# Expert tiles of a mixture-of-experts layer handled in pairs

## The chip, the cores and the metric

The kernel runs on one core of a Trainium2 chip. The metric is the device time of one execution in microseconds. Five engines work side by side, each through its own list of instructions: TensorE (PE, matrix products and transposes), VectorE (DVE), ScalarE (ACT), GpSimd (POOL) and SyncE (SP, which issues transfers). They wait for each other through semaphores: an instruction adds to one when it is done, and another engine waits until it has reached a count. Products land in eight PSUM banks of 128 partitions by 512 float32 words.

## The reference

The program is one decoder layer on 16 sequences of 128 tokens, 256 wide: self-attention, cross-attention, and a mixture of experts, each added to its input and normalized. The change touches the last of the three:

```
topk_idx, topk_w = _route(tokens, router_weight, router_bias)      # 4 of 32 experts for each token
gate_vals = silu(einsum('th,eih->tei', tokens, gate_w))            # i = 128
up_vals = einsum('th,eih->tei', tokens, up_w)
expert_out = einsum('tei,ehi->teh', gate_vals * up_vals, down_w)
mixed = (take_along_axis(expert_out, topk_idx) * topk_w).sum(1)
x = layernorm(x + mixed + shared)                                  # shared: one more expert for all tokens
```

Only the four chosen experts of a token are computed: 2048 tokens give 8192 rows of work.

## The kernel before

**Sorting.** While the stage before the experts still runs, POOL writes each token's row, with the place where its result belongs and its weight, to a DRAM table `x_rows` that is sorted by expert (indirect stores, L1390).

**Tiles.** `expert_layer` then goes through the table in tiles of 128 rows, all of one expert. The first 32 tiles are the first 128 rows of each expert ("by expert": which expert is known when the program is built). What an expert has beyond that is handled in 63 further tiles "by table": a small table is computed on the chip, and PE and SP read each tile's expert and row from registers. NT is 95 tiles. Numbers are kept as two float16 parts, a high and a low one (`_hi`, `_lo`), and a product is three matmuls.

**One step.** Each engine runs through steps i, and in a step does its part for tiles of different age, by the lags of the diff:

- SP fetches a tile's rows into one of G = 15 buffers `xg` (L2077).
- PE, in this order: the gate and up products of tile i - 3 (by table L2282, six matmuls of 256 columns; by expert L2251, twelve of 128); by table the transpose of tile i - 5's product `eh` (L2292); four transposes of tile i's rows (L2300); the down product of tile i - 8 (by expert i - 7), three matmuls (L2311).
- ACT: the copy of the transposed rows to `gT` (L2118), the high part `eh_hi` (L2123 by expert, L2127 by table), the silu of the gate (L2132).
- DVE: the result `yo` out of PSUM (by expert L2191, which multiplies by the row's weight; by table L2193, a copy), the rows' destinations `ix` (L2197), the low part `eh_lo` (L2201), the product `eh` of silu and up (L2210 by expert; L2213 by table, where the weight is applied).
- POOL: for each tile, when `yo` and `ix` are there, one indirect store of 128 rows to their places in `y_rows` (L2093).

The order on each engine is written out by hand: each function has its steps one after the other, and an engine waits in that order.

**PSUM.** Gate and up use banks 0 to 2, the down product banks 3 and 4; a tile's transposed rows and the transposed `eh` of another tile share one of the banks 5 to 7, which is why ACT waits for `ehlo_r` ahead of its copy and for `gt_ps` ahead of `eh_hi`:

```
if by_table(n - L_TR):
    act.wait_ge(ehlo_r, n - L_TR + 1)
act.activation(gT[:, n % U], GT_BANK[n % len(GT_BANK)], ACT.Copy).then_inc(gt_r, 1)
```

**After the tiles.** When all stores have landed, SP reads `y_rows` back (L2084), POOL and DVE add a token's four results, PE adds the residual (L2319), and the last normalization follows.

Of the kernel before, what the change touches and what calls it, by code (L numbers as in the profile page):

```python
# [35 lines left out]
LATE_PADS = {8: (16, 24), 15: (24, 32)}  # L36
PAD_PARTS = 16
ROUTE_SCALE = 2.5
NT = NE + NB * TOPK - 1
# [1922 lines left out]
def expert_layer(nc, c, st, consts, out):  # L1962
# [34 lines left out]
    with ExitStack() as before_tail:  # L1997
        def s3t(name, shape, dt=F32):
            return before_tail.enter_context(nc.sbuf_tensor(name, shape, dt))

        ix = s3t("ix", [P, IX, 1], U32)
        yo = c.front[:, 8 * D:8 * D + 2 * YO * D].bitcast(F32).rearrange("p (q d) -> p q d", q=YO)
        gT = s3t("gT", [P, U, 2, KT, P], F16)
        eg = c.front[:, 8 * D + 2 * YO * D:8 * D + 2 * YO * D + 2 * U * EI].bitcast(F32).rearrange("p (u w) -> p u w", u=U)
        eh = s3t("eh", [P, U, EI])
        eh_hi = s3t("eh_hi", [P, U, EI], F16)
        eh_lo = s3t("eh_lo", [P, U, EI], F16)

    words = c.xT[:].rearrange("p n s k t -> p (n s k t)").bitcast(U32)
    xg = words[:, 0:G * RW].rearrange("p (g w) -> p g w", g=G)  # L2010
# [14 lines left out]
    dn_ps, yo_r = sem("dn_ps"), sem("yo_r")  # L2025
    stored = [sem(f"stored{k}") for k in range(YO)]
# [5 lines left out]
    TAB_BANK = banks[4]  # L2032
# [6 lines left out]
    def xg_word(dt, q, w):  # L2039
        return xg[:, q, D + w:D + w + 1].bitcast(dt)  # L2040
# [4 lines left out]
    def by_expert(n):  # L2045
        return live(n, NE)

    def by_table(n):
        return NE <= n < NT

# [3 lines left out]
    def on_sync(sp, read_up_to, pad_rows):  # L2054
# [4 lines left out]
        for n in range(NT):  # L2059
# [10 lines left out]
            if n < G:  # L2070
                read_up_to((4 * RW * (n + 1) - 1) // (2 * 2 * KT * P))
            if by_expert(n - G):
                sp.wait_ge(yo_r, n - G + 1)
            elif by_table(n - G):
                sp.wait_ge(eh_r, n - G + 1)
                sp.wait_ge(ix_r, n - G + 1)
            sp.dma_start(xg[:, n % G], c.x_rows[bass.ds(rows[n % REGS] if n >= NE else rows[n], P), :]).then_inc(gathered[n % G], 16)  # L2077

        for q in range(YO):
            sp.wait_ge(stored[q], 16 * len(range(q, NT, YO)))  # L2080
# [29 lines left out]
    def on_scalar(act):  # L2110
        def tile(i, s, h):
            n = i - L_GT
            if live(n, NT):
                act.wait_ge(gt_ps, n + 1)
                wait(act, gu_ps, n - U + 1)
                if by_table(n - L_TR):
                    act.wait_ge(ehlo_r, n - L_TR + 1)
                act.activation(gT[:, n % U], GT_BANK[n % len(GT_BANK)], ACT.Copy).then_inc(gt_r, 1)  # L2118
            for n in due(i, L_HI):
                wait(act, dn_ps, n - U + 1)  # L2120
                if by_expert(n):
                    act.wait_ge(eh_r, n + 1)
                    act.activation(eh_hi[:, n % U], eh[:, n % U], ACT.Copy).then_inc(ehhi_r, 1)  # L2123
                else:
                    act.wait_ge(tr_ps, n - NE + 1)
                    act.wait_ge(gt_ps, min(n + L_TR + 1, NT))
                    act.activation(eh_hi[:, n % U], TR_BANK[(n + L_TR) % len(TR_BANK)], ACT.Copy).then_inc(ehhi_r, 1)  # L2127
            n = i - L_SILU
            if live(n, NT):
# [4 lines left out]
        unrolled(LAG3, tile, NT)  # L2134
# [46 lines left out]
    def on_vector(dve):  # L2181
        def tile(i, s, h):
# [4 lines left out]
            for n in due(i, L_YO):  # L2187
                dve.wait_ge(dn_ps, n + 1)
                wait(dve, stored[n % YO], 16 * (n // YO))
# [4 lines left out]
            n = i - L_IX  # L2194
            if live(n, NT):
                dve.wait_ge(gathered[n % G], 16 * (n // G + 1))
                dve.tensor_copy(ix[:, n % IX], xg_word(U32, n % G, 0)).then_inc(ix_r, 1)  # L2197
            for n in due(i, L_HI):
                dve.wait_ge(ehhi_r, n + 1)
                wait(dve, dn_ps, n - U + 1)  # L2200
                dve.tensor_tensor(eh_lo[:, n % U], eh[:, n % U] if by_expert(n) else TR_BANK[(n + L_TR) % len(TR_BANK)], eh_hi[:, n % U], ALU.subtract).then_inc(ehlo_r, 1)  # L2201
            n = i - L_SILU
            if live(n, NT):
                dve.wait_ge(eg_r, n + 1)
                if by_expert(n - U):
                    dve.wait_ge(ehlo_r, n - U + 1)
                elif by_table(n - U):
                    dve.wait_ge(tr_ps, n - U - NE + 1)
# [169 lines left out]
```

## Time and profile before

| | |
|---|---|
| runs | 769.65, 769.81, 773.45 us; median 769.81 |
| profiled execution | span 771.7 us; its own time is not listed apart |
| busy: PE | 602.3 us, 78% of the span |
| busy: DVE | 517.8 us, 67% |
| busy: ACT | 484.5 us, 63% |
| busy: POOL | 474.2 us, 61% |
| expert tiles | 549 to 729 us of the span, the last part of it from 729 to 771 |

Busy time is the time in which an engine executes something; waiting is not in it. The shares are means over the whole program, whose stages have different limits; the expert tiles are 180 of the 771.7 us. A released wait shows in the timeline as idle time in square brackets ahead of an instruction, with the one that ended it. Releasers are inferred: of several semaphores waited for, the last to arrive is named. "issue" is time in which the engine waited for nothing that the profile shows.

### The profile page before, as it was taken

The page shows a single profiled execution, that of the slowest core. Times are in us where ns is not written, and L with a number is a line of the kernel's source. Part 1 is how long each engine was busy: PE and PEld are TensorE (multiplying, and loading weights), DVE is VectorE, ACT ScalarE, POOL GpSimd, SP SyncE. Part 2 cuts the span into 40 slices and gives each one's busy share as a digit, 9 for nine tenths or more (in the row PEclk, how much of TensorE's full clock was granted, in tenths as well). Part 3 has the DMA queues.
Part 4 walks back from the last instruction along what each step waited for, and adds up shares of the span by engine and source line. Part 5 has one row for each costly group of instructions (what it writes and reads, how often), then busy time and mean ns, then how long its engine had stood idle before and what let it go on. Part 6 is the DMA issues. An engine that isn't in the chain of part 4 may idle for free.

```text
span 771.7 us, 24579 instructions
## 1 busy us (share of the span) xinstructions
PE 602.3 (78%) x8258; PEld 489.9 (63%) x8258; DVE 517.8 (67%) x2067; ACT 484.5 (63%) x1325; POOL 474.2 (61%) x622
## 2 busy tenths in 40 slices
PE   2899999999997568888778877563787777777383
PEld 1678989888886546566556655452776666566262
DVE  3988999988885236999999765452554545454374
ACT  3889999998997337777777654511455555454122
POOL 4758999999898713448667534542055555455583
PEclk9999999999998769999999868767999999999788
DMA  9310000001000022345554522347443454442193
GB/s 294 107 27 3 3 2 3 3 15 50 2 3 2 1 70 71 104 151 159 176 166 145 180 89 70 103 147 217 134 122 110 110 157 140 131 135 77 51 360 145
DMA packets 53641, 77.81 MB, mean 101 GB/s; under 512 B 8456, under 2 KB 42512, under 8 KB 52880
## 3 DMA queue, kind: packets, MB, share of 16 engines
q1 hardware_dynamic: 42768, 56.50, 25.1%
q0 software_dynamic: 7632, 16.87, 6.1%
q10 hardware_dynamic: 3120, 2.88, 1.1%
q8 instruction: 69, 1.13, 0.6%
q14 instruction: 52, 0.43, 0.2%
HBM read 48.62 MB, written 27.49 MB: 99 GB/s over the span
## 4 chain that ended last, share of the span: by engine, by line
PE 25%; DVE 15%; issue 11%; another core or an unknown queue 4%; ACT 4%; POOL 3%; DMA 1%; DVEq 0%; ACTq 0%; POOLq 0%; SPq 0%
PE bank L2311 6%; PE bank L2282 4%; DVE mnx L1541 3%; PE bank L2300 2%; PE bank L1766 2%; PE bank L1838 2%; PE bank L2251 2%; PE bank L2292 1%; PE bank L1919 1%; PE bank L1841 1%; DVE eh L2213 1%; PE bank L1815 1%; POOL ya L2101 1%; DVE we_lo L1581 1%
## 5 line engine op out<-in xcount | busy, mean ns | idle before, releaser
L2093 POOL DMA_INDIRECT y_rows<-front,ix x95 | 93.5, 984 | 106.8 <-DVE ix L2197 82.6
L566 ACT ACTIVATE sc<-sc,mn 128x128 f32<-128x128 f32 x256 | 82.5, 416 | 2.2 <-DVE mn L785 2.2
L1390 POOL DMA_INDIRECT x_rows<-rows,slot_ix x64 | 64.8, 1012 | 21.3 <-issue 13.2
L2118 ACT ACTIVATE gT<-bank 128x512 f16<-128x512 f16 x95 | 56.4, 595 | 29.5 <-DVE eh_lo L2201 12.6
L785 DVE CUSTOM_DVE_ANT_0 sc<-bank,rel 128x128 f32<-128x128 f32 x256 | 57.6, 285 | 0.8 <-issue 0.5
L2193 DVE COPY front<-bank 128x256 f32<-128x256 f32 x63 | 26.4, 419 | 43.5 <-PE bank L2311 43.2
L794 DVE TENSOR_TENSOR pT_lo<-bank,pT_hi 128x512 f16<-128x512 f32 x64 | 43.1, 675 | 5.1 <-ACT pT_hi L573 5.0
L1455 ACT ACTIVATE pT<-bank 128x512 f32<-128x512 f32 x64 | 33.9, 597 | 15.3 <-PE bank L1841 13.0
L969 PE MATMUL bank<-hT,w_hi 128*128 128x128 f16 x384 | 42.4, 224 | 1.2 <-POOL hT L376 0.9
L1541 DVE TENSOR_REDUCE mnx<-bank 128x4 f32<-128x512 f32 x64 | 39.7, 682 | 5.3 <-PE bank L1815 5.2
L1766 PE MATMUL bank<-w_hi,front 128*128 128x256 f16 x120 | 26.4, 322 | 19.3 <-DVE front L1707 19.3
L573 ACT ACTIVATE pT_hi<-bank 128x512 f16<-128x512 f32 x64 | 38.5, 603 | 4.5 <-PE bank L928 4.2
L2127 ACT ACTIVATE eh_hi<-bank 128x128 f16<-128x128 f32 x63 | 17.3, 274 | 37.5 <-PE bank L2311 36.8
L2282 PE MATMUL bank<-we_hi,gT 128*128 x252 | 37.9, 273 | 3.1 <-issue 2.2
L928 PE MATMUL bank<-ident,sc 128*128 128x128 f32 x256 | 39.4, 276 | 1.1 <-DVE k_lo L775 1.1
L2292 PE MATMUL bank<-ident,eh 128*128 128x128 f32 x63 | 17.8, 283 | 26.6 <-DVE eh L2213 25.8
L2300 PE MATMUL bank<-ident,hT 128*128 128x128 f16 x380 | 37.1, 219 | 1.6 <-DVE front L2191 0.7
L1497 ACT ACTIVATE front<-bank 128x256 f32<-128x256 f32 x16 | 6.0, 383 | 50.5 <-PE bank L1919 26.2
L1364 POOL TENSOR_TENSOR we_lo<-east,we_hi 128x256 f16<-128x256 f32 x48 | 31.2, 681 | 7.7 <-ACT we_hi L1423 7.4
L1372 POOL TENSOR_SCALAR xvar<-xmv 128x1 f32<-128x1 f32 x16 | 3.6, 226 | 52.4 <-DVE xmv L1605 52.4
L1838 PE MATMUL bank<-front 32*128 32x128 f16 x768 | 32.1, 228 | 2.7 <-issue 2.4
L2191 DVE TENSOR_SCALAR front<-bank,hT 128x256 f32<-128x256 f32 x32 | 15.3, 480 | 27.0 <-remote 17.0
(318 smaller groups left out, 2403.4 us busy)
## 6 DMA issues: line engine op xcount, KB each, us to landing
east<-in_experts SPq DMA_DIRECT2D x32, 384.0 KB
hT<-x_rows SPq DMA_DIRECT2D x95, 129.0 KB
rows<-xhl SPq DMA_DIRECT2D x16, 512.0 KB, 3.8
hT<-y_rows SPq DMA_DIRECT2D x16, 512.0 KB, 5.3
x_rows<-pad_block SPq DMA_DIRECT2D x32, 129.0 KB, 2.9
wst<-in_wcat SPq DMA_DIRECT2D x8, 256.0 KB, 6.8
front<-in_ctx_t SPq DMA_DIRECT2D x16, 128.0 KB, 2.9
out<-fin ACTq DMA_DIRECT2D x16, 128.0 KB, 5.0
```

Source lines behind the costliest of these rows:

```text
L566: done = act.activation(sc[:, g, j], sc[:, g, j], ACT.Exp, bias=mn[:, n % 2, g, j:j + 1], scale=-1.0)
L785: dve.tensor_tensor_reduce(out=sc[:, g, j], in0=sc_bank[g][:, j * P:(j + 1) * P], in1=rel[:, g, j], scale=-1.0, scalar=-NEG, op0=ALU.add, ...
L794: dve.tensor_tensor(pT_lo[:, g % 2], pT_bank[g][:].rearrange("p (h k) -> p h k", h=GH), pT_hi[:, g % 2], ALU.subtract).then_inc(pT_rd[g], 1)
L969: last = pe.matmul(room[u][:, m * P:(m + 1) * P], w[:, k, col + m * P:col + (m + 1) * P], hT[:, n, hp, k], start=t == 0 and not bias, stop ...
L1390: pool.indirect_dma_start(shared.x_rows, bass.IndirectOffsetOnAxis(ap=slot_ix[:, n, k:k + 1], axis=0), rows4[:, q, k], None).then_inc(shar ...
L1541: dve.tensor_reduce(mnx[:, n % 2, g], sc_bank[g][:].rearrange("p (h k) -> p h k", h=GH), AX_X, ALU.min).then_inc(xmn_r[g], 1)
L1838: pe.matmul(scT_bank[j][:, at], kk[r, s, m, b], qq[r, s, m], start=t == 0, stop=False)
L2093: pool.indirect_dma_start(c.y_rows, bass.IndirectOffsetOnAxis(ap=ix[:, n % IX], axis=0), yo[:, n % YO], None, bounds_check=NDEST - 1, oob_ ...
L2118: act.activation(gT[:, n % U], GT_BANK[n % len(GT_BANK)], ACT.Copy).then_inc(gt_r, 1)
L2282: done = pe.matmul(GU_BANK[n % len(GU_BANK)][:, 0:2 * EI].rearrange("p (m w) -> p m w", m=2), gT[:, n % U, x_, k], E[y_][k][:, :, bass.ds( ...
L2300: done = pe.transpose(GT_BANK[n % len(GT_BANK)][:, part, k], xg.bitcast(F16)[:, n % G, (part * KT + k) * P:(part * KT + k + 1) * P], c.ide ...
L2311: done = pe.matmul(DN_BANK[n % 2][:, 0:D].rearrange("p (h w) -> p h w", h=2), H[x_][:, n % U], E[y_][KT][:, :, bass.ds(e, EI)], start=t == ...
```

## The change

All engines handle two tiles in a step. NT becomes 96, that is 48 pairs, of which 16 are by expert. PE still does each tile's matmuls and transposes, but both tiles' results lie side by side in one PSUM bank and are signalled once; ACT copies, rounds and applies silu once for a pair (128x1024, 128x256, 128x256 for twice 128x512, 128x128, 128x128), DVE makes the low part, the destinations and, by table, the output copy once for a pair (128x256, 128x4, 128x512). Where the row's weight is applied, DVE keeps one instruction a tile. Gate and up have the banks 0 and 1, the down product 3 and 4, the transposed rows 5 and 6, the transposed `eh` 2 and 7: rows and `eh` no longer share a bank, and ACT's two waits for that are gone. The destinations and weights are copied out of the fetched rows early, so a fetch waits for the transposes and that copy only (`gt_ps`, `ix_r`), and not for the outputs (`yo_r`) or the products (`eh_r`). POOL waits once for a pair and then issues two stores as before. The lags are counted in pairs, and are smaller.

```
-NT = NE + NB * TOPK - 1
+NT = NE + NB * TOPK
...
-    U = 6
-    G = 15
-    IX = 20
-    YO = 8
+    NPAIR, NEPAIR = NT // 2, NE // 2
+    U = 3
+    G = 7
+    IX = 12
+    YO = 4
     REGS = 16
-    L_IX = 2
-    L_GT, L_GU, L_SILU, L_TR = 2, 3, 4, 5
-    L_HI, L_DN, L_YO = (5, 6), (7, 8), (8, 9)
+    L_GT, L_GU, L_SILU, L_TR = 1, 2, 3, 4
+    L_HI, L_DN, L_YO = (4, 5), (5, 6), (6, 7)
...
-    GT_BANK = [b[:].bitcast(F16)[:, 0:2 * D].rearrange("p (s k t) -> p s k t", s=2, k=KT) for b in banks[5:8]]
-    TR_BANK = [b[:, D:D + P] for b in banks[5:8]]
-    GU_BANK, DN_BANK = banks[0:3], banks[3:5]
+    GT_BANK = [b[:].bitcast(F16).rearrange("p (h s k t) -> p h s k t", h=2, s=2, k=KT) for b in banks[5:7]]
+    GU_BANK = [b[:].rearrange("p (h m w) -> p h m w", h=2, m=2) for b in banks[0:2]]
+    TR_BANK = [b[:, 0:2 * P].rearrange("p (h t) -> p h t", h=2) for b in (banks[2], banks[7])]
+    DN_BANK = [b[:].rearrange("p (h d) -> p h d", h=2) for b in banks[3:5]]
...
-            if by_expert(n - G):
-                sp.wait_ge(yo_r, n - G + 1)
-            elif by_table(n - G):
-                sp.wait_ge(eh_r, n - G + 1)
-                sp.wait_ge(ix_r, n - G + 1)
-            sp.dma_start(xg[:, n % G], c.x_rows[bass.ds(rows[n % REGS] if n >= NE else rows[n], P), :]).then_inc(gathered[n % G], 16)
+            wait(sp, gt_ps, p - G + 1)
+            wait(sp, ix_r, p - G + 1)
+            sp.dma_start(xg[:, p % G, h], c.x_rows[bass.ds(rows[n % REGS] if n >= NE else rows[n], P), :]).then_inc(gathered[p % G], 16)
...
-        for n in range(NT):
+        for n in range(NPAIR):
             pool.wait_ge(yo_r, n + 1)
-            pool.wait_ge(ix_r, n + 1)
-            pool.indirect_dma_start(c.y_rows, bass.IndirectOffsetOnAxis(ap=ix[:, n % IX], axis=0),
-                                    yo[:, n % YO], None, bounds_check=NDEST - 1, oob_is_err=False).then_inc(stored[n % YO], 16)
+            for h in range(2):
+                pool.indirect_dma_start(c.y_rows, bass.IndirectOffsetOnAxis(ap=ix[:, n % IX, h, 0:1], axis=0),
+                                        yo[:, n % YO, h], None, bounds_check=NDEST - 1, oob_is_err=False).then_inc(stored[n % YO], 16)
...
-                if by_table(n - L_TR):
-                    act.wait_ge(ehlo_r, n - L_TR + 1)
-                act.activation(gT[:, n % U], GT_BANK[n % len(GT_BANK)], ACT.Copy).then_inc(gt_r, 1)
+                act.activation(gT[:, n % U], GT_BANK[n % 2], ACT.Copy).then_inc(gt_r, 1)
...
-                act.activation(eg[:, n % U], GU_BANK[n % len(GU_BANK)][:, 0:EI], ACT.Silu).then_inc(eg_r, 1)
+                act.activation(eg[:, n % U], GU_BANK[n % 2][:, :, 0], ACT.Silu).then_inc(eg_r, 1)
...
-                    dve.tensor_scalar(yo[:, n % YO], DN_BANK[n % 2][:, 0:D], xg_word(F32, n % G, 1), None, ALU.mult).then_inc(yo_r, 1)
+                    dve.tensor_scalar(yo[:, n % YO, 0], DN_BANK[n % 2][:, 0], row_weight(n, 0), None, ALU.mult).then_inc(yo_half, 1)
+                    dve.tensor_scalar(yo[:, n % YO, 1], DN_BANK[n % 2][:, 1], row_weight(n, 1), None, ALU.mult).then_inc(yo_r, 1)
                 else:
-                    dve.tensor_copy(yo[:, n % YO], DN_BANK[n % 2][:, 0:D]).then_inc(yo_r, 1)
+                    dve.tensor_copy(yo[:, n % YO], DN_BANK[n % 2]).then_inc(yo_r, 1)
...
-                dve.tensor_copy(ix[:, n % IX], xg_word(U32, n % G, 0)).then_inc(ix_r, 1)
+                dve.tensor_copy(ix[:, n % IX], xg[:, n % G, :, D:D + 2]).then_inc(ix_r, 1)
...
-                pe.transpose(TR_BANK[i % len(TR_BANK)], eh[:, n % U], ident[:]).then_inc(tr_ps, 1)
+                for q in range(2):
+                    done = pe.transpose(TR_BANK[n % 2][:, q], eh[:, n % U, q], ident[:])
+                done.then_inc(tr_ps, 1)
```

The order on the engines changes in three places that matter below. First PE, in the part by table: before, a step is one tile, down product (L2311), gate and up (L2282), transposes of `eh` (L2292) and of the next rows (L2300).

```order
L2292 MATMUL bank<-ident,eh 128x128
L2300 MATMUL bank<-ident,hT 128x128 x4
L2311 REGISTER_ALU
L2311 MATMUL bank<-we_hi,eh_hi 128x256
L2311 MATMUL bank<-we_hi,eh_lo 128x256
L2311 REGISTER_ALU
L2311 MATMUL bank<-we_lo,eh_hi 128x256
L2282 ISA
L2282 MATMUL bank<-we_hi,gT 128x256
```

With the change the same place on PE reads (gate and up, now L2274, stand ahead of and behind these rows, twice in a row):

```order
L2286 MATMUL bank<-ident,eh 128x128 x2
L2295 MATMUL bank<-ident,hT 128x128 x8
L2305 REGISTER_ALU
L2305 MATMUL bank<-we_hi,eh_hi 128x256
L2305 MATMUL bank<-we_hi,eh_lo 128x256
L2305 REGISTER_ALU
L2305 MATMUL bank<-we_lo,eh_hi 128x256
L2305 REGISTER_ALU
L2305 MATMUL bank<-we_hi,eh_hi 128x256
L2305 MATMUL bank<-we_hi,eh_lo 128x256
L2305 REGISTER_ALU
L2305 MATMUL bank<-we_lo,eh_hi 128x256
```

Every kind stands in the same order as before, twice in a row, so PE comes back to a kind after two tiles' work instead of one.

Next DVE, where the part by expert passes into that by table; before (`front` is the memory in which `yo` and the silu lie, `hT` that of the fetched rows), two steps by table:

```order
L2201 TENSOR_TENSOR eh_lo<-bank,eh_hi 128x128
L2213 SCALAR_TENSOR_TENSOR eh<-bank,hT,front 128x128
L2193 COPY front<-bank 128x256
L2197 COPY ix<-hT 128x1
L2201 TENSOR_TENSOR eh_lo<-bank,eh_hi 128x128
L2213 SCALAR_TENSOR_TENSOR eh<-bank,hT,front 128x128
```

With the change, from the last pair by expert to the second by table:

```order
L2186 TENSOR_SCALAR front<-bank,front 128x256
L2187 TENSOR_SCALAR front<-bank,front 128x256
L2194 COPY front<-hT 128x4
L2198 TENSOR_TENSOR eh_lo<-bank,eh_hi 128x256
L2211 SCALAR_TENSOR_TENSOR eh<-bank,front 128x128 x2
L2194 COPY front<-hT 128x4
L2198 TENSOR_TENSOR eh_lo<-bank,eh_hi 128x256
L2211 SCALAR_TENSOR_TENSOR eh<-bank,front 128x128 x2
L2189 COPY front<-bank 128x512
```

Output copy, destinations and low part are one wide instruction for two tiles, the weighted ones (L2186 with L2187, L2211) stay two of the old width.

Last POOL, from the last indirect stores into `x_rows` through those of the tiles to the first sum behind them; semaphore numbers are used again, so that the name before (`mixhi_r`) stands for `yo_r`:

```order
L1390 DMA x_rows<-rows,slot_ix 69760x258 x3
L1390 DMA x_rows<-rows,slot_ix 69760x258 [waits sc_part0,khi_r,ln_rstd]
L1390 DMA x_rows<-rows,slot_ix 69760x258 x3
L2093 DMA y_rows<-front,ix 8192x256 [waits ix_r,mixhi_r] x95
L2101 TENSOR_TENSOR ya<-hT 128x256 [waits y_in0]
```

With the change (`lwhi_r` stands for `yo_r`) the stores begin:

```order
L2092 DMA y_rows<-front 8192x256 [waits lwhi_r]
L2092 DMA y_rows<-front 8192x256
L2092 DMA y_rows<-front 8192x256 [waits lwhi_r]
L2092 DMA y_rows<-front 8192x256
L2092 DMA y_rows<-front 8192x256 [waits lwhi_r]
```

POOL's stores stand in the same place; each waited for two semaphores, now every second one waits for one.

## Rows read from the trace of the kernel before

**Rows 1.** Table of windows, two stretches of the part by table (columns in its first line).
```profile
core 0: us, PE busy (x) PEld busy (x) DVE busy (x) ACT busy (x) POOL busy (x), PEclk, DMA share, GB/s
630.00:640.00 10.00, 7.09 (x72) 5.84 (x71) 4.82 (x21) 4.74 (x16) 4.92 (x5) 1.00 0.44 131
700.00:710.00 10.00, 7.12 (x74) 6.10 (x72) 4.75 (x22) 4.89 (x15) 5.05 (x6) 1.00 0.16 55
```

**Rows 2.** Timeline from 672.5 us (start, duration, engine, line, operation, [idle before <-releaser]).
```profile
674.36 0.42 DVE L2193 COPY front<-bank 128x256 f32<-128x256 f32 x1 [2.29 <-PE bank L2311]
...
675.55 0.98 POOL L2093 DMA_INDIRECT y_rows<-front,ix  x1 [2.08 <-DVE ix L2197]
...
676.02 0.27 PE L2311 MATMUL bank<-we_lo,eh_hi 128*128 x1
...
676.42 0.41 DVE L2193 COPY front<-bank 128x256 f32<-128x256 f32 x1
...
678.13 0.98 POOL L2093 DMA_INDIRECT y_rows<-front,ix  x1 [0.30 <-issue]
...
678.65 0.27 PE L2311 MATMUL bank<-we_lo,eh_hi 128*128 x1
...
679.99 0.42 DVE L2193 COPY front<-bank 128x256 f32<-128x256 f32 x1 [2.28 <-PE bank L2311]
680.02 0.28 ACT L2127 ACTIVATE eh_hi<-bank 128x128 f16<-128x128 f32 x1 [1.86 <-PE bank L2311]
...
681.19 0.98 POOL L2093 DMA_INDIRECT y_rows<-front,ix  x1 [2.07 <-DVE ix L2197]
```

**Rows 3.** Timeline of the expert stage, first transposes on PE and stores on POOL.
```profile
549.04 0.61 PE L2300 MATMUL bank<-ident,hT 128*128 128x128 f16 x8
...
557.92 1.00 POOL L2093 DMA_INDIRECT y_rows<-front,ix  x1 [29.91 <-DVE ix L2197]
...
593.69 0.98 POOL L2093 DMA_INDIRECT y_rows<-front,ix  x1 [2.04 <-DVE ix L2197]
...
599.30 0.98 POOL L2093 DMA_INDIRECT y_rows<-front,ix  x1 [2.04 <-DVE ix L2197]
...
616.27 0.98 POOL L2093 DMA_INDIRECT y_rows<-front,ix  x1 [1.87 <-DVE ix L2197]
...
719.64 0.98 POOL L2093 DMA_INDIRECT y_rows<-front,ix  x1 [1.21 <-issue]
...
727.37 0.98 POOL L2093 DMA_INDIRECT y_rows<-front,ix  x1 [0.30 <-issue]
```

**Rows 4.** Timeline of the indirect stores into x_rows, 498 to 531 us.
```profile
500.21 0.96 POOL L1390 DMA_INDIRECT x_rows<-rows,slot_ix  x1 [0.30 <-issue]
...
509.07 0.96 POOL L1390 DMA_INDIRECT x_rows<-rows,slot_ix  x1 [0.30 <-issue]
...
511.91 0.66 ACT L1497 ACTIVATE front<-bank 128x256 f32<-128x256 f32 x2 [8.26 <-remote]
```

**Rows 5.** Chain that ended last, 676 to 682 us (start, us, what).
```profile
677.28 0.33 PE bank L2311 x3
677.61 0.66 PE bank L2282 x6
678.26 0.11 PE bank L2292
678.37 0.22 PE bank L2300 x4
```

**Rows 6.** Groups by line, expert stage (xcount | busy, mean ns | idle before, releasers).
```profile
L2118 ACT ACTIVATE gT<-bank 128x512 f16<-128x512 f16 x95 | 56.4, 595 | 29.5 <-DVE eh_lo L2201 12.6 <-PE bank L2300 7.0 <-issue 5.4
...
L2191 DVE TENSOR_SCALAR front<-bank,hT 128x256 f32<-128x256 f32 x32 | 15.3, 480 | 27.0 <-remote 17.0 <-PE bank L2311 10.0
```

**Rows 7.** The page's costliest groups of instructions, two lines with other widths.
```profile
L1541 DVE TENSOR_REDUCE mnx<-bank 128x4 f32<-128x512 f32 x64 | 39.7, 682 | 5.3 <-PE bank L1815 5.2
...
L1497 ACT ACTIVATE front<-bank 128x256 f32<-128x256 f32 x16 | 6.0, 383 | 50.5 <-PE bank L1919 26.2
```

More of the change, by code:

```diff
@@ L2045, in by_expert @@
     def by_expert(n):
-        return live(n, NE)
+        return live(n, NEPAIR)
     def by_table(n):
-        return NE <= n < NT
+        return NEPAIR <= n < NPAIR
     def due(i, lags):
@@ L2181, in on_vector, with pair_step @@
     def on_vector(dve):
-        def tile(i, s, h):
+        def pair_step(i, s, h):
             if i == L_GU + 2:
@@ L2244, in on_tensor, with pair_step @@
     def on_tensor(pe, shared_done):
-        def products(o, lhs, rhs, tiles, width):
-            for m in range(tiles):
-                t = 0
-                for x_, y_ in ((0, 0), (0, 1), (1, 0)):
-                    for k in range(KT):
-                        done = pe.matmul(o[:, m * width:(m + 1) * width], lhs(x_, k, m), rhs(y_, k, m),
-                                         start=t == 0, stop=t == 5)
-                        t += 1
-            return done
         owners = [e * EI for e in range(NE)]
-        def tile(i, s, h):
+        def pair_step(i, s, h):
             if i == L_GU + 1:
@@ L2286, in tile @@
-            wait(pe, gt_r, min(i - len(GT_BANK) + 1, NT))
-            if by_table(i - len(TR_BANK) - L_TR):
-                pe.wait_ge(ehlo_r, i - len(TR_BANK) - L_TR + 1)
+                wait(pe, eh_r, n - 1)
+                for q in range(2):
+                    e, o, x = owners[2 * n + q], GU_BANK[n % 2][:, q], gT[:, n % U, q]
+                    if by_expert(n):
+                        for m in range(2):
+                            t = 0
+                            for x_, y_ in ((0, 0), (0, 1), (1, 0)):
+                                for k in range(KT):
+                                    done = pe.matmul(o[:, m], E[x_][k][:, m, bass.ds(e, EI)], x[:, y_, k], start=t == 0, stop=t == 5)
+                                    t += 1
+                    else:
+                        t = 0
+                        for x_, y_ in ((0, 0), (1, 0), (0, 1)):
+                            for k in range(KT):
+                                done = pe.matmul(o, x[:, x_, k], E[y_][k][:, :, bass.ds(e, EI)], start=t == 0, stop=t == 5)
+                                t += 1
@@ L2289, in tile @@
+                done.then_inc(gu_ps, 1)
             n = i - L_TR
             if by_table(n):
+                if n == NEPAIR:
+                    shared_done(banks[7])
+                    pe.wait_ge(tab_ready, 2)
+                if by_table(n - 2):
+                    pe.wait_ge(ehlo_r, n - 1)
                 pe.wait_ge(eh_r, n + 1)
-                pe.transpose(TR_BANK[i % len(TR_BANK)], eh[:, n % U], ident[:]).then_inc(tr_ps, 1)
+                for q in range(2):
+                    done = pe.transpose(TR_BANK[n % 2][:, q], eh[:, n % U, q], ident[:])
@@ L2293, in tile @@
+                done.then_inc(tr_ps, 1)
             n = i
[L2294 to L2301 removed]
+            if live(n, NPAIR):
+                pe.wait_ge(gathered[n % G], 32 * (n // G + 1))
+                wait(pe, gt_r, n - 1)
+                for q in range(2):
+                    for part in range(2):
+                        for k in range(KT):
+                            done = pe.transpose(GT_BANK[n % 2][:, q, part, k],
+                                                xg.bitcast(F16)[:, n % G, q, (part * KT + k) * P:(part * KT + k + 1) * P], c.ident16[:])
@@ L2307, in tile @@
                 wait(pe, yo_r, n - 1)
-                if n == 1:
-                    pe.wait_ge(tab_ready, 2)
-                for t, (x_, y_) in enumerate(((0, 0), (1, 0), (0, 1))):
-                    done = pe.matmul(DN_BANK[n % 2][:, 0:D].rearrange("p (h w) -> p h w", h=2), H[x_][:, n % U], E[y_][KT][:, :, bass.ds(e, EI)],
-                                     start=t == 0, stop=t == 2)
+                for q in range(2):
+                    e = owners[2 * n + q]
+                    for t, (x_, y_) in enumerate(((0, 0), (1, 0), (0, 1))):
+                        done = pe.matmul(DN_BANK[n % 2][:, q].rearrange("p (h w) -> p h w", h=2), H[x_][:, n % U, q], E[y_][KT][:, :, bass.ds(e, EI)],
+                                         start=t == 0, stop=t == 2)
                 done.then_inc(dn_ps, 1)
-        unrolled(LAG3, tile, NT)
+        unrolled(LAG3, pair_step, NPAIR)
         for n in range(NB):
```

100 lines of the change are left out of this document (40 added, 60 removed).

## Prediction

> **What bounds the kernel now.** The change touches the expert layer only, so I first looked for that stage in the table of windows [rows 1]. In both windows TensorE (PE) is busy for 7.1 of 10 us, VectorE (DVE), ScalarE (ACT) and GpSimd (POOL) for 4.7 to 5.1, and the granted clock is 1.00, the upper of its two levels (2.4 GHz). Nothing is full, so something makes the engines take turns. The second thing to see: at 700 to 710 us hardly anything is fetched any more and the DMA share is 0.16 instead of 0.44, yet PE does the same amount. Fetching is not the limit.
>
> The timeline shows the turns [rows 2]. POOL starts stores 1.29 us apart: 675.55, one between, 678.13; then none until 681.19. Three tiles in 5.64 us, 1.88 a tile. Inside the burst a hand-over is quick: the down product that starts at 676.02 and takes 0.27 is followed by DVE's output copy at 676.42, 0.13 us after its end. At the end of the burst it is not: the product of 678.65 is over at 678.92, but DVE starts at 679.99 and ACT at 680.02, in the same instant, though they wait for different things of PE. So for about a microsecond PE's signals don't arrive, and this ends 1.86 us after the start of the last store of the burst (678.13 to 679.99). Then DVE copies (0.42) and POOL starts 0.78 us after the copy's end. The round adds up: 2 x 1.29 + 1.86 + 0.42 + 0.78 = 5.64.
>
> That the stores hold the signals up, and not PE's work, has two witnesses. In the part by expert, whose products are split over more and shorter matmuls, the round is just as long: 593.69 to 599.30, 5.61 us for three stores [rows 3]. And earlier in the program, while POOL runs indirect stores back to back (eight, the first at 500.21, the last at 509.07), ACT waits 8.26 us for a signal that comes 2.84 us after the start of the last of them [rows 4]. What carries the signals no view shows.
>
> **The sum.** I count store starts [rows 3]: the first at 557.92, the first tile by table at 616.27 (32 tiles, 1.823 a tile), the last at 727.37. The last six intervals, where PE has little left, are 1.29 each (719.64 to 727.37); the 56 before them take 103.4 us, 1.846 each.
>
> *What stays.* PE's work per tile: 0.33 + 0.66 + 0.11 + 0.22 = 1.32 us by table [rows 5], 2.64 a pair. POOL's: two stores a pair as before, 2.58. Rows fetched: two DMAs a pair, issued earlier than now, and off the path. One tile more (96 for 95).
>
> *What is merged.* Per pair ACT loses a copy and an activation of 128x512 and 128x128, and gets one twice as wide. From 256 to 512 columns ACT goes from 383 to 595 ns [rows 6, 7], so 1024 cost about 1.02 for 2 x 0.595; DVE's output copy of 512 columns costs 0.68 (the nearest row, a reduction over 512 columns of PSUM) for 2 x 0.42 [rows 2, 7]. By expert the copy stays two instructions of 0.48 [rows 6], and POOL waits for the second: 0.96. All of this is work of engines that are half idle, so as busy time I cost it at nothing. It counts only where it stands in the round: in the copy between release and next store.
>
> *The new round.* PE runs ahead until it needs something that a held-back signal would have to start; by the lags that is two steps beyond the last step that was heard, now and after the change: what PE transposes back at L_TR DVE has multiplied a step earlier, out of products that PE made two steps earlier at L_GU (5 and 3 now, 4 and 2 after). Now two steps are two tiles, and a third tile's product is over in time: after the release at 674.36 DVE works, and the down product whose last matmul starts at 676.02 is heard at once [rows 2], for the next burst has lasted less than a microsecond by then. After the change a step is 2.64 us and its ACT part alone 1.02 + 0.38 + 0.38, so the third step can't be heard in time. Two steps are then two pairs: a burst of four stores. Round by table: 3 x 1.29 + 1.86 + 0.68 + 0.78 = 7.19. One thing comes off: a store that is waited for starts 0.78 after the copy, one whose signals are there 0.30 after the store before it. The difference, 0.48, is two waits handled one after the other (outputs and indices); one of them goes. I take half, 0.24 (bounds 0 and 0.48). So 6.95 for four, 1.74 a tile. By expert 3 x 1.29 + 1.86 + 0.96 + 0.54 = 7.23, 1.81.
>
> *The start.* From the first transposes (549.04) to the first store (557.92) it is 8.9 us for a lag of 8 tiles [rows 3], 1.11 a step. Afterwards the lag is 6 pairs, and a step of twice the width takes some 1.71 times as long, as ACT's copy does (1.02 for 0.595): 6 x 1.11 x 1.71 = 11.4, 2.5 later (bounds 0 and, with a factor of 2, 4.4).
>
> Together: start +2.5; by expert 32 x (1.81 - 1.823) = -0.4; by table 57 intervals x 1.74 + 6 x 1.29 = 106.9 against 111.1, -4.2. Sum -2.1 us. The span of the profile, 771.7, becomes 769.6; it lies 1.9 us (0.25%) above the median of the runs, 769.8, and takes the place of the profiled execution's own time, which is not listed apart. Against the median I say **768 us**.
>
> **The rivals.** *The signals get through between the pairs.* PE sends four signals a pair instead of eight, ACT three instead of six, so fewer queue behind a held one; and if the second pair's copy is late, the burst breaks after two stores and the signals come through there. Then the pace lies between PE's 1.32 and the round's 1.74; at the middle, 1.53 by table and 1.5 by expert, the sum is 2.5 - 10.3 - 16.2 = -24: 746 us. At PE's own pace it would be 728. For it: inside a burst some signals do pass now, since PE's second step is fed during it. Against it: PE and POOL need almost the same per pair (2.64 and 2.58), so stores bunch by themselves, as they do now; and the burst of eight held ACT up for 8.26 us.
>
> *Only one pair per release.* Slower, by one mechanism: during a burst the second pair's low part and activation need signals between ACT, DVE and PE; if these are held too, PE does only one more pair before the release, and a round of two stores takes 1.29 + 1.86 + 0.68 + 0.54 = 4.37, 2.19 a tile. It decides as soon as the second pair's down product misses the release. Rounds of four and two in turn give 1.89 a tile by table and 1.98 by expert: 2.5 + 4.2 + 5.0 = +12, 782 us; nothing but rounds of two gives 809. For it: the pause grows with each instruction that stands between release and first store, and the pair's are all longer. Against it: PE's second step does get what it needs during a burst now.
> This is the direction of a rule of the Trainium skill (Perfetto Trace Analysis, Optimizing Scalar/DVE Operations): wider operations help where the engine is saturated; where ScalarE and VectorE are not, but cause bubbles elsewhere, breaking instructions up may let work finish sooner. By that rule this change goes the wrong way, for here the two engines are half idle and PE has the bubbles. The trace bears the rule's condition out, but puts the bubble down to late signals and not to long instructions, so I give it no more than the chance of this rival.
>
> *Nothing moves:* the bursts stay three tiles' worth by some other limit. Then only the start and one tile more (1.85) count: 1.85 to 4.4, 772 to 774.
>
> **Chances.** About 0.5% (3.85 us) is what a measurement of this kernel can tell from no change: 766 to 773.7 is "same". The forecast's round of four: 0.47, its own range 760 to 777 from the bounds of the wait, the copy and the start; of this 0.15 faster, 0.24 same, 0.08 slower. Signals through between pairs: 0.29, faster. One pair per release, wholly or in turn: 0.18, slower. Nothing moves: 0.06, same. So 0.44 faster, 0.30 same, 0.26 slower. The range of 744 to 786 leaves out the fast end of the one rival and the slow end of the other, some 0.2 together.
>
> **What would show it.** In the changed profile: POOL's stores in bursts of four at 1.29 with a pause, about 7 us from burst to burst, in the part by expert as in that by table; DVE's copy and ACT's step released together about 1.9 us after the start of the fourth store; ACT's wide copy near 1.0 us, DVE's near 0.68; the first store near 560.4. It is wrong if pauses stand after every second store, if POOL runs on without pauses, or if the stores' spacing widens evenly: then signals are not held by bursts as I read it. A stage that is shorter with the same rounds of four would mean that the release itself comes sooner.

## The result, and the profile after

The changed kernel takes 780.36 us (median of 4 runs, 778.25 to 782.58) where the kernel before took 769.73 in the same comparison: ratio 1.0115, interval 1.0081 to 1.0150. Repeated with 12 runs beside 17 of before it was 1.0070 (1.0044 to 1.0095). So it is slower, by 0.7 to 1.2%, and the forecast of 768 us with its range of 744 to 786 had the sign wrong: 0.44 of the chance stood on faster, 0.26 on slower.

Of the two profiled executions (spans 771.7 and 780.8 us) only a part is the change. The last indirect store into `x_rows`, ahead of the expert stage and in code that the change doesn't touch, starts at 527.05 before and at 531.22 after. The table of windows shows one stretch where they differ, 310 to 320 us, first the kernel before and then the changed one; the granted clock is 1.00 and 0.74:

```profile
core 0: us, PE busy (x) PEld busy (x) DVE busy (x) ACT busy (x) POOL busy (x), PEclk, DMA share, GB/s
310.00:320.00 10.00, 8.44 (x172) 6.23 (x171) 9.38 (x36) 7.74 (x22) 4.26 (x8) 1.00 0.30 83
310.00:320.00 10.00, 9.24 (x142) 7.20 (x139) 5.68 (x13) 6.85 (x17) 3.13 (x7) 0.74 0.21 57
```

In the profiles of the twelve further runs below the same stretch shows anything from 0.60 to 1.00 and the last of those stores starts between 522.9 and 530.7 us, with the same instructions up to there; ten of them run variants of the changed kernel, and these spread over the whole range. I take that for scatter and not for the change, and therefore count from the first transposes of the expert stage to its last store: 178.3 us before [rows 3]; after, in the timeline (start, duration, engine, line):

```profile
552.99 1.06 PE L2295 MATMUL bank<-ident,hT 128*128 128x128 f16 x16
...
565.58 1.00 POOL L2092 DMA_INDIRECT y_rows<-front  x1 [33.40 <-DVE front L2187]
...
617.83 0.98 POOL L2092 DMA_INDIRECT y_rows<-front  x1 [2.35 <-DVE front L2187]
...
621.70 0.99 POOL L2092 DMA_INDIRECT y_rows<-front  x1 [0.30 <-issue]
...
627.18 0.98 POOL L2092 DMA_INDIRECT y_rows<-front  x1 [4.49 <-DVE front L2189]
...
736.47 0.99 POOL L2092 DMA_INDIRECT y_rows<-front  x1 [0.30 <-issue]
```

736.47 - 552.99 = 183.5 us, 5.2 more than before, and 185.3 in the repetition: 0.7 to 0.9% of the time, which is what the repeated ratio says. Behind the last store both executions need 44.3 us.

Inside the stage the forecast's picture holds. The timeline of one round by table, the counterpart of [rows 2]:

```profile
675.74 0.98 POOL L2092 DMA_INDIRECT y_rows<-front  x1 [2.44 <-DVE front L2189]
...
677.03 0.99 POOL L2092 DMA_INDIRECT y_rows<-front  x1 [0.30 <-issue]
...
678.32 0.99 POOL L2092 DMA_INDIRECT y_rows<-front  x1 [0.30 <-issue]
...
679.26 0.27 PE L2305 MATMUL bank<-we_lo,eh_hi 128*128 x1
...
679.61 0.99 POOL L2092 DMA_INDIRECT y_rows<-front  x1 [0.30 <-issue]
...
681.48 1.02 ACT L2115 ACTIVATE gT<-bank 128x1024 f16<-128x1024 f16 x1 [4.24 <-remote]
...
681.55 0.69 DVE L2189 COPY front<-bank 128x512 f32<-128x512 f32 x1 [3.57 <-remote]
...
683.02 0.99 POOL L2092 DMA_INDIRECT y_rows<-front  x1 [2.42 <-DVE front L2189]
```

Four stores 1.29 us apart, then a pause, 7.28 us from burst to burst. The down product that ends at 679.53 is copied at 681.55, two microseconds later; ACT and DVE go on within 0.07 us of each other, 1.87 and 1.94 us after the start of the fourth store. The releaser reads "remote": the profile finds none near, because the signal arrived so long after the matmul that sent it. The trace also has the moment at which a semaphore was raised: PE's for this product at 681.53, two microseconds after its end and 0.02 before the copy. So the signal is late, not the engine that waits for it. (Two earlier signals of PE come through during the burst, at 678.49 and 679.23, for work that ends at 678.21 and 678.43.) The wide instructions have the lengths that were forecast (about 1.02 and 0.68 us), in the groups by line of the expert stage [rows 6]:

```profile
L2115 ACT ACTIVATE gT<-bank 128x1024 f16<-128x1024 f16 x48 | 49.3, 1029 | 96.1 <-remote 85.0 <-PE bank L2295 7.9 <-issue 3.2
...
L2189 DVE COPY front<-bank 128x512 f32<-128x512 f32 x32 | 22.0, 688 | 54.2 <-remote 44.1 <-PE bank L2305 10.1
```

### The profile page after: what moved, and what is told of

Its sections match the earlier page's. It is cut to its first block, busy times and chain, and to the rows that moved or that the text cites. A ratio compares the mean times of both kernels' runs of the same rounds, so it can differ in the third digit from the quotient of the medians.

```text
span 780.8 us, 23930 instructions
## 1 busy us (share of the span) xinstructions
PE 610.4 (78%) x8272; PEld 497.1 (64%) x8272; DVE 504.6 (65%) x1927; ACT 466.4 (60%) x1184; POOL 477.4 (61%) x623
## 4 chain that ended last, share of the span: by engine, by line
PE 22%; DVE 12%; issue 11%; ACT 8%; another core or an unknown queue 6%; POOL 4%; DMA 1%; ACTq 0%; DVEq 0%; POOLq 0%; SPq 0%
PE bank L2274 6%; PE bank L1766 3%; DVE mnx L1541 2%; PE bank L2305 2%; ACT gT L2115 2%; PE bank L1919 2%; PE bank L1838 2%; ACT eh_hi L2122 1%; PE bank L2295 1%; PE bank L2268 1%; POOL ya L2100 1%; DVE we_lo L1581 1%; ACT front L2127 1%; PE bank L1815 1%
## 5 line engine op out<-in xcount | busy, mean ns | idle before, releaser
L2092 POOL DMA_INDIRECT y_rows<-front x96 | 95.6, 996 | 109.6 <-DVE front L2187 52.2
L2115 ACT ACTIVATE gT<-bank 128x1024 f16<-128x1024 f16 x48 | 49.3, 1029 | 96.1 <-remote 85.0
L2274 PE MATMUL bank<-we_hi,gT 128*128 x256 | 39.7, 278 | 26.9 <-ACT gT L2115 20.5
L2189 DVE COPY front<-bank 128x512 f32<-128x512 f32 x32 | 22.0, 688 | 54.2 <-remote 44.1
L2274 PEld LDWEIGHTS bank<-we_hi,gT 128*128 128x128 f16 x256 | 24.0, 99 | 34.5 <-issue 31.9
L952 PE MATMUL bank<-w_hi,hT 128*128 128x256 f16 (+1 forms) x128 | 31.8, 331 | 0.3 <-DVE vlin L737 0.3
L1423 ACT ACTIVATE we_hi<-east 128x256 f16<-128x256 f32 (+1 forms) x80 | 31.4, 461 | 0.0
L2135 ACT ACTIVATE fin<-bank,fshift,frstd 128x256 f32<-128x256 f32 x16 | 9.0, 565 | 37.4 <-DVE fshift L2238 26.6
```

The lines of the kernel that those rows point to most:

```text
L2115: act.activation(gT[:, n % U], GT_BANK[n % 2], ACT.Copy).then_inc(gt_r, 1)
L2274: done = pe.matmul(o, x[:, x_, k], E[y_][k][:, :, bass.ds(e, EI)], start=t == 0, stop=t == 5)
```

## The experiments

"The changed kernel" and "before" stand for the two kernels of the case; ratios are to before, measured beside it on the same chip.

**1. The stores taken off POOL.** In both kernels SP stores the tiles with plain transfers, in its loop behind the fetch of a later tile or pair; the indirect stores, and with them the places of the results, are left out. In the changed kernel:

```
-                pool.indirect_dma_start(c.y_rows, bass.IndirectOffsetOnAxis(ap=ix[:, n % IX, h, 0:1], axis=0),
-                                        yo[:, n % YO, h], None, bounds_check=NDEST - 1, oob_is_err=False).then_inc(stored[n % YO], 16)
...
+        sp.wait_ge(yo_r, n + 1)
+        for h in range(2):
+            r = (2 * n + h) % (NDEST // P) * P
+            sp.dma_start(c.y_rows[r:r + P, :], yo[:, n % YO, h]).then_inc(stored[n % YO], 16)
```

> The changed kernel with its indirect stores left out: SP stores each tile with a plain transfer to fixed rows of y_rows (pair p - 12 behind the fetch of pair p), so the results don't reach their tokens. Theory A, POOL's indirect stores hold the signals up: ACT and DVE follow PE within about 0.2 us, no common releases, PE sets the pace at 1.32 to 1.5 us a tile, and the time falls by 30 to 45 us. Theory B, the pair's longer chain of copies sets the round, stores or not: 1.7 to 1.85 a tile, the time falls by less than 10 us.

> The kernel before with its indirect stores left out in the same way (tile n - 20 behind the fetch of tile n). Theory A (stores hold the signals up): also PE's pace, 1.32 to 1.5 a tile, 30 to 45 us less than before; then both kernels differ by the start (3.7 us) and little else, and merging pays nothing where PE is the limit. Theory B (what bounds is the number of hand-overs): b_plain is slower than a_plain by 10 us or more.

Measured: changed kernel 721.6 us, ratio 0.930 (0.924 to 0.937); before 728.3 us, 0.937 (0.929 to 0.944). The table of windows of the former, one stretch by expert and one by table:

```profile
core 0: us, PE busy (x) PEld busy (x) DVE busy (x) ACT busy (x) POOL busy (x), PEclk, DMA share, GB/s
570.00:580.00 10.00, 10.00 (x157) 9.71 (x156) 6.46 (x20) 6.65 (x13) 0.00 (x0) 1.00 0.59 173
640.00:650.00 10.00, 10.00 (x110) 9.24 (x108) 6.23 (x20) 5.78 (x13) 0.00 (x0) 1.00 0.76 224
```

PE is busy without a gap, where it had 7.1 of 10 us [rows 1]. Theory A is borne out, and by more than it expected for the changed kernel: the indirect stores cost it some 59 us (ratio 1.0070, see 7, to 0.930) and the kernel before 45. Without them PE alone sets the pace. Merging by itself is no loss, where the expectation had the two kernels apart by the start only: from the first transposes to the last down product the paired kernel now needs 127.9 us and the other 133.0 (in the latter DVE waits 10 us for SP's stores, so not all of the 5 us is due to merging).

**2. What in a store holds the signals.** Two kernels, one run each. In the first POOL issues plain transfers to fixed rows, so the indices play no part; in the second the indirect stores move half of each row.

```
-                pool.indirect_dma_start(c.y_rows, bass.IndirectOffsetOnAxis(ap=ix[:, n % IX, h, 0:1], axis=0),
-                                        yo[:, n % YO, h], None, bounds_check=NDEST - 1, oob_is_err=False).then_inc(stored[n % YO], 16)
+                pool.dma_start(c.y_rows[r:r + P, :], yo[:, n % YO, h]).then_inc(stored[n % YO], 16)
```

```
-                pool.indirect_dma_start(c.y_rows, bass.IndirectOffsetOnAxis(ap=ix[:, n % IX, h, 0:1], axis=0),
-                                        yo[:, n % YO, h], None, bounds_check=NDEST - 1, oob_is_err=False).then_inc(stored[n % YO], 16)
+                pool.indirect_dma_start(c.y_rows.rearrange("n (s d) -> (n s) d", s=2), bass.IndirectOffsetOnAxis(ap=ix[:, n % IX, h, 0:1], axis=0),
+                                        yo[:, n % YO, h, 0:P], None, bounds_check=NDEST - 1, oob_is_err=False).then_inc(stored[n % YO], 16)
```

> The changed kernel with POOL's stores as plain transfers to fixed rows of y_rows (the indices aren't used, so results don't reach their tokens), still issued by POOL. Theory A, it is POOL's making of a transfer that holds PE's signals, whatever its address: bursts and common releases as now, time within 10 us of the changed kernel. Theory B, only the indirect form holds them: no common releases, 1.25 to 1.4 us a tile, as when SP issues the stores, 40 to 55 us less.

> The changed kernel, but each indirect store moves 128 of a row's 256 columns (128 descriptors as before, half the bytes), to half-rows of y_rows; the other half of the results is left out, and y_rows is read back from its first half only. Theory A, the hold goes by the descriptors: stores 1.29 apart, release 1.85 to 1.95 after the last one's start, rounds of 7.2 to 7.3. Theory B, it goes by the bytes that the store moves: release after 1.3 to 1.6, rounds of 6.6 to 7.0, and 4 to 10 us less over the stage.

Measured: 727.27 us with plain stores, 52.5 less than the changed kernel beside it (779.79), theory B: POOL's stores come in pairs every 2.44 us by expert and 2.63 by table, 1.2 to 1.3 us a tile. The groups by line of its expert stage show POOL's stores at 0.54 us, and ACT's copy waiting for PE alone, no "remote":

```profile
L2093 POOL DMA_DIRECT2D y_rows<-front x96 | 51.4, 540 | 99.6 <-DVE front L2187 53.9 <-DVE front L2189 44.3 <-issue 1.3
L2115 ACT ACTIVATE gT<-bank 128x1024 f16<-128x1024 f16 x48 | 49.0, 1023 | 47.5 <-PE bank L2295 47.5
```

With half rows the time is as before, 780.58 us, theory A. In its timeline the stores take 0.98 us, and ACT is released 1.94 us after the fourth:

```profile
683.28 0.98 POOL L2092 DMA_INDIRECT y_rows<-front  x1 [2.53 <-DVE front L2189]
...
687.14 0.98 POOL L2092 DMA_INDIRECT y_rows<-front  x1 [0.31 <-issue]
...
689.08 1.02 ACT L2115 ACTIVATE gT<-bank 128x1024 f16<-128x1024 f16 x1 [4.30 <-remote]
```

So it is the indirect form that holds PE's signals, not its bytes, and not that POOL issues it. What of the indirect form does it, the runs don't separate; whether the hold goes by the number of rows was not tried.

**3. Air between the stores.** A POOL copy behind each store, of one column in the first kernel and of 128 in the second (shown).

```
+                wait(pool, paced, 2 * n + h)
+                pool.tensor_copy(pace, c.ident[:]).then_inc(paced, 1)
```

> The changed kernel with a copy of one column on POOL behind each store (about 0.23 us), so that stores inside a burst are some 1.6 us apart instead of 1.29. Theory A, what holds PE's signals up is the stores' crowding: with air between them the signals come through inside a burst, the bursts of four dissolve into stores about evenly spaced, 1.6 to 1.75 us a tile, 7 to 20 us less. Theory B, each burst holds the signals from its first store to about 1.9 us after its last one, however the stores are spaced: a round of four grows by 3 x 0.3, from 7.28 to about 8.2, and the time by 20 us.

> The changed kernel with a POOL copy of 128 columns behind each store; the one of a single column fitted into the gap and moved the stores only from 1.29 to 1.34 us. Now some 1.55 to 1.65 apart. Theory A, with air between the stores PE's signals come through inside a burst: bursts dissolve, 1.6 to 1.75 us a tile. Theory B, signals are held from about 1 us after the first store to 1.9 after the last, however they are spaced: rounds of four at 8.1 to 8.4 us, 15 to 25 us slower.

Measured: ratios 1.0101 (1.0047 to 1.0155) and 1.0157 (1.0096 to 1.0219). The first tells nothing: its copy ran in the gap that was there, and the stores moved only to 1.34 us. In the second they are 1.45 apart, less than meant. Its timeline:

```profile
681.44 0.98 POOL L2093 DMA_INDIRECT y_rows<-front  x1 [1.73 <-DVE front L2192]
...
682.42 0.30 POOL L2096 COPY front<-ident 128x128 f32<-128x128 f32 x1
...
682.89 0.98 POOL L2093 DMA_INDIRECT y_rows<-front  x1 [0.17 <-issue]
...
685.80 0.98 POOL L2093 DMA_INDIRECT y_rows<-front  x1 [0.17 <-issue]
...
687.39 1.02 ACT L2118 ACTIVATE gT<-bank 128x1024 f16<-128x1024 f16 x1 [4.33 <-remote]
...
688.93 0.98 POOL L2093 DMA_INDIRECT y_rows<-front  x1 [1.85 <-DVE front L2192]
```

The bursts of four stay, against theory A; but the round grows by 0.2 us at most (7.49 for 7.28, or for the 7.38 of the repetition in 7) and not by 3 x 0.16, since the release now comes 1.59 us after the last store. Neither theory had this. It helps to count from the first store of a burst. The kernel before has a round of two stores, and the burst of [rows 4] begins one store ahead of the row shown, so it has nine and not eight (timeline of the kernel before):

```profile
498.92 0.98 POOL L1390 DMA_INDIRECT x_rows<-rows,slot_ix  x1 [0.16 <-issue]
...
644.59 0.98 POOL L2093 DMA_INDIRECT y_rows<-front,ix  x1 [2.08 <-DVE ix L2197]
...
645.88 0.98 POOL L2093 DMA_INDIRECT y_rows<-front,ix  x1 [0.31 <-issue]
...
647.64 0.42 DVE L2193 COPY front<-bank 128x256 f32<-128x256 f32 x1 [0.90 <-PE bank L2311]
```

The release comes 3.0 us after the first of two stores, 4.4 for three (675.55 to 679.99 in [rows 2]), 5.7 for four, 6.0 for these spread four, and 13.0 for the nine (498.92 to 511.91): 1.4 to 1.5 us for each store. That looks like a piece of work of that length per store, lined up one behind the other, with PE's signals behind it. If so, a spacing of 1.45 is hardly wider than that work and could open no gap. Wider spacing was not tried, and what the work is no view shows. Not every burst fits: by expert some bursts of three in the kernel before are released after 3.6 us already (566.98 to 570.59).

**4. The wide output copy.** Two copies of one tile each; POOL starts the first store when the first half is there.

```
-                    dve.tensor_copy(yo[:, n % YO], DN_BANK[n % 2]).then_inc(yo_r, 1)
+                    dve.tensor_copy(yo[:, n % YO, 0], DN_BANK[n % 2][:, 0]).then_inc(yo_half, 1)
+                    dve.tensor_copy(yo[:, n % YO, 1], DN_BANK[n % 2][:, 1]).then_inc(yo_r, 1)
...
-            pool.wait_ge(yo_r, n + 1)
             for h in range(2):
+                pool.wait_ge((yo_half, yo_r)[h], n + 1)
```

> The changed kernel, but the output copy of a pair by table is two copies of 256 columns, and POOL starts a pair's first store when the first tile's copy is done (by expert too). Theory A, the copy stands in the round between the release of the signals and the next store: a round by table falls from 7.28 to 7.01 us (0.42 for 0.69), by expert from 7.46 to 7.06 (0.48 for 0.88); 16 and 8 rounds, -7.5 us against the changed kernel. Theory B, the round is set by the chain through ACT and PE, the copy runs beside it: rounds stay at 7.28 and 7.46, the time within 2 us. Theory C, an earlier store shortens the stretch in which signals get through, and the second pair misses it: rounds of two appear, slower by 5 us or more.

Measured: ratio 1.0008 (0.9973 to 1.0042), where the changed kernel has 1.0070. Rounds are 7.1 by table and 7.2 by expert, the stage 180.2 us (183.5, and 185.3 in the repetition): theory A in kind, though only half to two thirds of the 7.5 us expected, for the release comes later (673.65 is 2.05 us after the fourth store):

```profile
667.73 0.98 POOL L2092 DMA_INDIRECT y_rows<-front  x1 [2.25 <-DVE front L2190]
...
671.60 0.99 POOL L2092 DMA_INDIRECT y_rows<-front  x1 [0.30 <-issue]
...
673.65 0.42 DVE L2189 COPY front<-bank 128x256 f32<-128x256 f32 x1 [3.34 <-remote]
...
674.85 0.98 POOL L2092 DMA_INDIRECT y_rows<-front  x1 [2.25 <-DVE front L2190]
```

**5. The passage from one part to the other.** The same lags in both.

```
-    L_HI, L_DN, L_YO = (4, 5), (5, 6), (6, 7)
+    L_HI, L_DN, L_YO = (5, 5), (6, 6), (7, 7)
```

> The changed kernel with one set of lags for both parts (high part 5, down product 6, output copy 7 pairs; by expert it had 4, 5, 6). Theory A, the pause of 5.48 us and the round of two stores where the part by expert passes into that by table come from the lags changing by a pair: both vanish, -3.2 us (6 tiles in 14.1 us become 6 at 1.82), and the first store comes one step later, +2.1 (12.6 us for six steps now): -1 us in all. Theory B, the pause is the wait for the table's registers: it stays, +2 us.

Measured: ratio 1.0027 (0.9989 to 1.0065), the stage 184.5 us. The pause of 5.48 us and the round of two are gone: the last round by expert starts at 611.64 and the first by table at 618.99, 7.35 us like any other. Theory A, for the passage. What it saves is paid at the front (first store 14.4 us after the first transposes for 12.6), and the rounds are no shorter (about 7.5 by expert, 7.3 by table); the stage gains nothing. The ratio is below the changed kernel's 1.0070, but the intervals overlap.

**6. The place of POOL's wait.** In the changed kernel two register moves stand on POOL ahead of a pair's first store, and the wait written ahead of the store is attached to the first of them: they start at 682.28 and 682.80, the store at 683.02. (In the kernel before it is one move with the wait for the outputs, then the wait for the indices: 680.45, 680.98, store at 681.19.) Here the wait for the outputs is attached to the store.

```
-            pool.wait_ge(yo_r, n + 1)
             for h in range(2):
-                pool.indirect_dma_start(c.y_rows, bass.IndirectOffsetOnAxis(ap=ix[:, n % IX, h, 0:1], axis=0),
-                                        yo[:, n % YO, h], None, bounds_check=NDEST - 1, oob_is_err=False).then_inc(stored[n % YO], 16)
+                store = pool.indirect_dma_start(c.y_rows, bass.IndirectOffsetOnAxis(ap=ix[:, n % IX, h, 0:1], axis=0),
+                                                yo[:, n % YO, h], None, bounds_check=NDEST - 1, oob_is_err=False)
+                if h == 0:
+                    store.wait_op(yo_r, n + 1, "sem-ge")
+                store.then_inc(stored[n % YO], 16)
```

> The changed kernel; only the place of POOL's wait is different: on the indirect store itself instead of on the first of the two register moves ahead of it, so that the moves are done before the outputs are there. Theory A, the 0.78 us between copy and store is POOL's own work behind the wait (0.52 to the second move, 0.22 to the store), and it stands in each round: rounds of 7.28 to 7.35 us become about 6.8, some 24 rounds, -10 to -12 us against the changed kernel. Theory B, the store comes earlier, but so does the hold of PE's signals; the chain through ACT and PE (PE works 5.6 us in a round and waits for ACT's second wide copy) then misses it: rounds stay at 7.2 or more, within 3 us.

> The late wait together with the output copies split by tile. Theory A: both savings add, rounds by table about 6.6 (7.10 - 0.5), by expert 6.75, -13 to -16 us against the changed kernel and 6 to 10 us under the kernel before. Theory B, the chain through ACT and PE sets a floor of about 7.1 that the split copy has reached already: no more than 3 us beyond the split copy alone.

> The kernel before with the late wait alone. Theory A, the round of three stores falls from 5.64 by 0.5 to about 5.15: some 31 rounds, -12 to -16 us against before, 1.6 to 2.0 percent. Theory B, the third tile's product, which is heard only because it comes early in the burst, is missed when the burst starts sooner: rounds of two (1.29 + 1.86 + 0.42 + 0.28 = 3.85, 1.93 a tile) appear, time within 1 percent or slower.

Measured: changed kernel 772.27 us, ratio 0.9969 (0.9940 to 0.9998); with the split copy 766.33, 0.9902 (0.9864 to 0.9941); the kernel before 764.36, 0.9885 (0.9845 to 0.9925). Theory A in all three, with less than was expected in the first (8 us under the changed kernel, for 10 to 12) and the last (1.2%, for 1.6 to 2.0). The changed kernel with the late wait, timeline of a round:

```profile
674.88 0.99 POOL L2091 DMA_INDIRECT y_rows<-front  x1 [0.30 <-issue]
...
676.88 1.02 ACT L2117 ACTIVATE gT<-bank 128x1024 f16<-128x1024 f16 x1 [3.86 <-remote]
...
676.95 0.69 DVE L2191 COPY front<-bank 128x512 f32<-128x512 f32 x1 [3.19 <-remote]
...
677.92 0.98 POOL L2091 DMA_INDIRECT y_rows<-front  x1 [2.05 <-DVE front L2191]
```

From the end of the copy (677.64) to the store it is 0.28 us instead of 0.78, and rounds by table are about 6.9; by expert they fall to 7.2 only. In the kernel before the round of three falls from 5.64 to 5.17; rounds of two, which theory B expected, occur five times where there were three, at 3.5 to 3.7 us:

```profile
671.05 0.98 POOL L2092 DMA_INDIRECT y_rows<-front,ix  x1 [1.64 <-DVE ix L2197]
672.34 0.99 POOL L2092 DMA_INDIRECT y_rows<-front,ix  x1 [0.30 <-issue]
673.63 0.98 POOL L2092 DMA_INDIRECT y_rows<-front,ix  x1 [0.30 <-issue]
676.22 0.98 POOL L2092 DMA_INDIRECT y_rows<-front,ix  x1 [1.61 <-DVE ix L2197]
```

The kernel before with the late wait and the changed one with late wait and split copy beat both kernels of the case; their intervals overlap, so which of them is the faster stays open.

**7. The changed kernel again.**

> The changed kernel once more, on this chip. Theory A, the change acts in the expert stage alone, which by the two profiles is 5.2 us longer from the first transposes to the last store: ratio 1.004 to 1.009. Theory B, the earlier stages, which ended 4 us later in its profiled execution, are slower with it too: ratio 1.011 to 1.015.

Measured: 1.0070 (1.0044 to 1.0095), theory A: what the change does to the time, it does, as far as this interval tells, in the expert stage.

## Why the prediction was wrong

*What bounds the kernel: right.* Indirect stores hold PE's signals; without them PE has no gap left (1). That it is the indirect form alone (2) the prediction had not said. Its second witness, the burst of [rows 4], has nine stores and not eight; the wait that it shows is the same.

*The new round: right in kind.* Bursts of four, in both parts, with a common release 1.87 to 1.94 us after the fourth store by table and 1.7 to 1.9 by expert, and instructions of the forecast widths.

*The new round's size: wrong, in the term of half of 0.48 us.* The prediction put the 0.48 between copy and store down to "two waits handled one after the other", and took half of it off since one wait goes. Nothing came off: 682.24 to 683.02 is 0.78 as before. The second wait went, but a second register move stands in its place: half a microsecond lies between the move that has the first wait and what follows it, before as after, and it goes when the wait is put on the store (6). The sign of the forecast hung on this term: with its lower bound, 0, the prediction's own sum is 2.5 + 1.4 - 0.9 = +3.0 us. With 0 and the measured release and copy the round by table is 3 x 1.29 + 1.94 + 0.69 + 0.78 = 7.28, the measured one; by expert it is 7.46 (52.25 us for the seven rounds from 565.58 to 617.83) where 7.23 stood. That is 1.82 and 1.87 us a tile against 1.85 and 1.82 before: four stores in a round, but a longer copy ahead of it, and the gain by table of 4.2 us shrinks to 1.8 (109.3 us from 627.18 to 736.47, for 111.1).

*The passage between the parts: not in the sum at all.* By expert 32 tiles take 61.6 us (565.58 to 627.18) where the sum had 0.4 less than the 58.35 of before: 3.3 more. Of this 1.4 is the rounds (eight times 7.46 against 7.29 for four tiles before), 1.9 the last round, 9.35 us long. The lags grow by a step there, and a step is now a pair; with equal lags the pause vanishes (5). In the kernel before such a step was one tile.

*The start: too small.* 12.6 us for 8.9, so +3.7 instead of +2.5, within the bounds of 0 to 4.4. Together 3.7 + 3.3 - 1.8 = +5.2 where the sum had -2.1.

*The rivals.* The measured time lies beside the 782 us of "only one pair per release", but not by that mechanism: rounds of two occur once, at the passage. A time that fits a rival is not yet the rival. "Signals through between the pairs" was given 0.29 and didn't come about; nor did it with 0.16 us more between the stores (3). The Trainium skill's rule (Perfetto Trace Analysis, Optimizing Scalar/DVE Operations), that breaking instructions up may let work finish sooner where ScalarE and VectorE aren't full, was given no more than the 0.18 of the first of these rivals, since the bubble came from late signals. Both are true: the late signal makes the pause, and the wide copy behind it lengthens the pause; splitting it, and letting the first store go at the first half, gave 3.3 to 5.1 us of the stage back (4).

## What to carry to other kernels

In a round of waits only what stands between the release and the next start counts: merging two instructions there costs what the second one takes, though both engines are half idle, while a wait moved behind its engine's preparations took 1.2% off the kernel before. When lags are counted in larger steps, each step that they grow by, at the start and wherever they change on the way, costs a larger step too. And before a price is guessed half-way between two bounds, it is worth finding out what the time consists of, above all when it is paid two dozen times.

## What the runs showed of the hardware that was not expected

- An indirect store of 128 rows (0.98 us on POOL, 1.29 from one to the next) holds up what PE signals, until 1.4 to 2.2 us after the last one's start in bursts of four; half the bytes change nothing. A plain store issued by POOL (0.54 us) or by SP doesn't. The changed kernel loses 52 to 59 us to it, the kernel before 45. Whether signals of other engines are held too these traces don't show: at the end of a burst ACT and DVE wait for PE alone.
- Counted from the first store of a burst the release comes in most bursts after 1.4 to 1.5 us for each store (two, three, four and nine stores), a little more than POOL's spacing of 1.29. Why, stays open.
- A register move ahead of an indirect store costs 0.5 us when it stands behind a wait (0.78 against 0.28 from copy to store).
- The granted clock of an earlier stage (0.60 to 1.00 at 310 to 320 us) differed between executions with the same instructions. The last store into `x_rows` started anywhere from 522.9 to 531.2 us, mostly late where that clock was low: more than the change itself is worth.
